# Softmax row sums folded by VectorE in 32-blocks instead of a running PSUM sum, in a one-core attention and FFN kernel

## The chip, the cores and the metric

The program runs on one core of one Trainium2 chip. The time is the device time of one execution in microseconds, the median of three runs. The engines are TensorE (PE, its weight loads are PEld), VectorE (DVE), ScalarE (ACT), GpSimd (POOL) and SyncE (SP, which issues the DMAs). Each engine executes its own instructions strictly in program order and waits for the others through semaphores.

## What is computed

One transformer layer over 2048 tokens of width 512, with 16 heads whose query and key have a 128-wide part without position and a 64-wide part with rotary position. All is float32.

```python
scores = jnp.einsum('bhqd,bhkd->bhqk', q_full, k_full) * scale
scores = jnp.where(causal, -jnp.inf, scores)
attn = jax.nn.softmax(scores.astype(jnp.float32), axis=-1)
out = jnp.einsum('bhqk,bhkd->bhqd', attn, v)
out = out.transpose(0, 2, 1, 3).reshape(b, s, H * DV)
x = _layernorm(x + out @ w_o.T)
x = _layernorm(x + ffn(x))          # w = weight * scale_weight[:, None];  x @ w.T + bias
```

The change concerns the denominator of the softmax: for each query the sum over its keys of the exponentials.

## The kernel before

The attention is worked off in 64 iterations `it`: 4 groups of 4 heads, and in each group the 16 query tiles of 128 tokens. An iteration visits `keys(it)` key tiles (1 to 16, causal), 544 in all. One visit is a slot. In a slot the data of four heads stand side by side: a tile has 128 partitions, which are the keys, and 4 x 128 columns, which are head and query. So a sum over keys is a sum over partitions and over the slots of the iteration.

A slot passes these steps, each on its engine:

- `scores`: five PE matmuls of 512 columns into one of two PSUM banks (`SCORES`, drawn as `rows`). PE may start slot n only when slot n - 2 has gone through `max`.
- `max` (steps `masked`, `max_of`): ACT copies the scores to a ring in SBUF (`pool`, L1606), and after that DVE joins them to a running maximum `top` (L1858). For the first slot of an iteration DVE adds the causal mask instead (L1847).
- `shift`: DVE adds the negated row maximum (L1873), `exp`: ACT (L1611).
- `sum` (`add_up`): DVE adds the exponentials to the running sum in PSUM bank `TOTAL` (L1885; a copy in the first slot, L1882).
- `hi`, `lo`: ACT (L1618) and POOL (L1730) split the exponentials into two parts, `values`: three PE matmuls of 512 columns (L1494, L1495, L1497) add them, times the values, to the bank `OUT`.

The values of a slot come six slots or more after its scores. Around the end of an iteration, `e` being the slot of its last values, there follow once per iteration: ACT copies `TOTAL` to SBUF (`copy_sum`, L1630); PE turns it by four 128x128 transposes (`turn_sum`, L1505); DVE reduces the turned tile over keys to 4 columns (L1889) and takes the reciprocal (L1892); PE spreads it back over the partitions by four more transposes of a broadcast column (`spread_sum`, L1513); DVE multiplies the output by it (`normalise`, L1897); ACT and POOL split the result (L1636, L1735); and 12 PE matmuls project it (`y`, L1527), whose result DVE adds to a partial sum in SBUF (L1836). The row maximum has a like pair of steps, `turn_max` (L1473) and `spread_max` (L1484). The projections of the queries (`q`, L1427, and `pe`, L1440) are made between the slots, for two iterations at a time.

The order on every engine comes from one list `STEPS`. `timetable()` gives each step a slot and a phase within the slot, and `plan()` sorts them and pulls forward what a step waits for. The results of `q`, `pe`, `y`, `turn_max`, `turn_sum`, `spread_sum` and of the two FFN products take turns in the `N_AUX` shared PSUM banks: a use waits until the readers of the use `N_AUX` places earlier are done. The FFN of a query tile follows in the last group, from slot `W_SLOT` on, nine or seven slots behind its last values.

Of the kernel before, what the change touches and what calls it, by code (L numbers as in the profile page):

```python
# [11 lines left out]
ALU = mybir.AluOpType  # L12
# [3 lines left out]
P = 128  # L16
# [646 lines left out]
N_SCORES, N_AUX = 2, 3  # L663
# [106 lines left out]
def timetable():  # L770

    for it in range(N_ITER):
# [55 lines left out]
def readers(use):  # L828
# [11 lines left out]
    if use[0] == "turn_sum":  # L840
        return [("reduce_sum", use[1])]
    if use[0] == "spread_sum":
        return [("normalise", use[1]), ("o_hi", use[1]), ("o_lo", use[1])]
# [16 lines left out]
def waits_for(step):  # L860
# [28 lines left out]
    elif what == "sum":  # L889
        yield ("exp", it, *rest)  # L890
        if it and rest[0] == 0:
            yield ("copy_sum", it - 1)
# [10 lines left out]
    elif what == "copy_sum":  # L903
        yield ("sum", *last_tile(it))
        if it:
            yield ("turn_sum", it - 1)
# [6 lines left out]
    elif what == "turn_sum":  # L913
        yield ("copy_sum", it)
    elif what == "reduce_sum":
        yield ("turn_sum", it)
        if it >= 2:
            yield ("spread_sum", it - 2)
    elif what == "spread_sum":
        yield ("reduce_sum", it)  # L920
# [96 lines left out]
AUX_USES = ("q", "pe", "y", "turn_max", "turn_sum", "spread_sum", "turn", "linear")  # L1017
# [72 lines left out]
def attention_phase(nc, m, block, x, bias, out):  # L1090


    with ExitStack() as ctx:
# [13 lines left out]
        total = sb("total", [P, 512])  # L1107
# [5 lines left out]
        sums = sb("sums", [P, 4, HG])  # L1113
# [17 lines left out]
        OUT, MAXES, TOTAL = m.bank[5:8]  # L1131
# [23 lines left out]
        sum_copied = sem("sum_copied")  # L1155
        sum_turned = sem("sum_turned")
        sum_done = sem("sum_done")
# [47 lines left out]
        def by_head(view):  # L1205

            return view.rearrange("p (h n) -> p h n", h=HG)

# [176 lines left out]
        def _(pe):  # L1385
            def wait_read(u):
# [9 lines left out]
                elif u[0] == "turn_sum":  # L1396
                    pe.wait_ge(sum_done, u[1] + 1)
# [157 lines left out]
            for what, *at in STEPS:  # L1555
# [10 lines left out]
                elif what == "turn_sum":  # L1566
                    turn_sum(*at)
                elif what == "spread_sum":
                    spread_sum(*at)
# [12 lines left out]
        def _(act):  # L1582
# [84 lines left out]
            for what, *at in STEPS:  # L1667
# [18 lines left out]
                elif what == "copy_out":  # L1686
                    copy_out(*at)
                elif what == "copy_sum":
                    copy_sum(*at)
                elif what == "o_hi":  # L1690
                    out_hi(*at)
# [102 lines left out]
        def _(dve):  # L1794
# [80 lines left out]
            def add_up(it, t):  # L1875
                n = number(it, t)
                dve.wait_ge(exp_done, n + 1)
                if t == 0:
                    if it:
# [152 lines left out]
```

## Time and profile before

| | |
|---|---|
| Median of three runs | 1715.34 us (1714.08 to 1717.51) |
| Profiled execution, its span from first to last instruction | 1714.7 us; it has no time of its own beside its span |
| PE busy | 1679.9 us, 98% |
| PEld busy | 1395.8 us, 81% |
| DVE busy | 1380.5 us, 81% |
| ACT busy | 1120.8 us, 65% |
| POOL busy | 979.7 us, 57% |

Busy times are unions: two instructions that overlap count once. Matmuls and DVE operations are pipelined, so a row's duration is longer than the distance to the next row's start. What an instruction takes of its engine is that distance, not its duration.

### The profile page before, as it was taken

The page shows a single profiled execution, that of the slowest core. Times are in us where ns is not written, and L with a number is a line of the kernel's source. Part 1 is how long each engine was busy: PE and PEld are TensorE (multiplying, and loading weights), DVE is VectorE, ACT ScalarE, POOL GpSimd, SP SyncE. Part 2 cuts the span into 40 slices and gives each one's busy share as a digit, 9 for nine tenths or more (in the row PEclk, how much of TensorE's full clock was granted, in tenths as well). Part 3 has the DMA queues.
Part 4 walks back from the last instruction along what each step waited for, and adds up shares of the span by engine and source line. Part 5 has one row for each costly group of instructions (what it writes and reads, how often), then busy time and mean ns, then how long its engine had stood idle before and what let it go on. Part 6 is the DMA issues. An engine that isn't in the chain of part 4 may idle for free.

```text
span 1714.7 us, 28541 instructions
## 1 busy us (share of the span) xinstructions
PE 1679.9 (98%) x8789; PEld 1395.8 (81%) x8789; DVE 1380.5 (81%) x2493; ACT 1120.8 (65%) x2128; POOL 979.7 (57%) x937
## 2 busy tenths in 40 slices
PE   7999999999999999999999999999999999999997
PEld 5567888888888888888888888888888888888775
DVE  3665788888888887878788888888888888888984
ACT  3564676666666676666677666766667777676774
POOL 4333465565555555655566555555556665556785
PEclk9999999999999999999999999999999999999999
DMA  7984322212321412223211413123123111111422
GB/s 204 367 330 136 105 68 62 87 56 88 110 80 37 144 36 81 69 80 117 81 62 44 142 50 92 51 80 114 62 66 105 56 57 62 50 44 44 136 92 80
DMA packets 112175, 164.03 MB, mean 96 GB/s; under 512 B 13600, under 2 KB 83488, under 8 KB 109984
## 3 DMA queue, kind: packets, MB, share of 16 engines
q1 hardware_dynamic: 105296, 125.86, 22.9%
q0 software_dynamic: 4864, 16.26, 3.0%
q10 hardware_dynamic: 1872, 20.19, 2.9%
q8 instruction: 68, 1.11, 0.3%
q14 instruction: 75, 0.61, 0.1%
HBM read 101.19 MB, written 61.08 MB: 95 GB/s over the span
## 4 chain that ended last, share of the span: by engine, by line
PE 89%; POOL 3%; DVE 3%; issue 2%; DMA 1%; ACT 1%; DVEq 0%; SPq 0%; ACTq 0%; POOLq 0%
PE rows L1464 35%; PE bank L1494 7%; PE bank L1497 7%; PE bank L1495 7%; PE rows L1527 7%; PE rows L1427 5%; PE bank L1527 3%; PE rows L392 2%; PE rows L1440 2%; PE bank L1427 2%; PE bank L1484 2%; PE bank L1440 1%; POOL split_p L1730 1%; PE rows L1473 1%; PE rows L1505 1%
## 5 line engine op out<-in xcount | busy, mean ns | idle before, releaser
L1730 POOL TENSOR_TENSOR split_p<-pool,split_p 128x512 fp32r<-128x512 f32 x544 | 703.3, 1294 | 503.2 <-ACT split_p L1618 503.1
L1464 PE MATMUL rows<-q_c,key_c 128*128 128x512 f32 x1632 | 477.0, 400 | 1.4 <-DVE top L1858 1.4
L1606 ACT COPY pool<-rows 128x512 f32<-128x512 f32 x480 | 281.8, 587 | 227.3 <-PE rows L1464 226.6
L1858 DVE TENSOR_TENSOR top<-rows,top 128x512 f32<-128x512 f32 x420 | 288.6, 687 | 124.5 <-ACT pool L1606 121.0
L1873 DVE TENSOR_TENSOR pool<-bank,pool 128x512 f32<-128x512 f32 x544 | 369.7, 680 | 19.8 <-PE bank L1484 19.8
L1611 ACT ACTIVATE pool<-pool 128x512 f32<-128x512 f32 x544 | 345.9, 636 | 18.1 <-DVE pool L1873 17.1
L1618 ACT CAST split_p<-pool 128x512 fp32r<-128x512 f32 x544 | 333.2, 612 | 16.7 <-PE bank L1497 16.7
L1464 PE MATMUL rows<-q_pe,key_pe 128*128 128x512 f32 x1088 | 337.1, 391 | 0.4 <-DMA q_pe<-pe_dram 0.4
L1885 DVE TENSOR_TENSOR bank<-bank,pool 128x512 f32<-128x512 f32 x480 | 330.9, 689 | 0.0
L1464 PEld LDWEIGHTS rows<-q_c,key_c 128*128 128x128 f32 x1632 | 288.0, 189 | 50.0 <-DVE top L1858 5.0
L1464 PEld LDWEIGHTS rows<-q_pe,key_pe 128*128 128x128 f32 x1088 | 204.2, 188 | 46.2 <-DMA q_pe<-pe_dram 0.9
L1497 PE MATMUL bank<-split_p,val 128*128 128x512 f32 x544 | 213.7, 393 | 2.9 <-POOL split_p L1730 2.7
L1494 PE MATMUL bank<-split_p,val 128*128 128x512 f32 x544 | 214.0, 393 | 1.5 <-ACT o_sum L1624 1.0
L1495 PE MATMUL bank<-split_p,val 128*128 128x512 f32 x544 | 212.3, 390 | 0.0
L1527 PE MATMUL rows<-wo,o_t 128*128 128x512 f32 x528 | 127.3, 390 | 0.4 <-ACT o_t L1636 0.4
L1497 PEld LDWEIGHTS bank<-split_p,val 128*128 128x128 f32 x544 | 102.1, 188 | 29.0 <-POOL split_p L1730 7.4
L1494 PEld LDWEIGHTS bank<-split_p,val 128*128 128x128 f32 x544 | 102.1, 188 | 25.9 <-ACT o_sum L1624 3.4
L1735 POOL TENSOR_TENSOR o_t<-o_sum,o_t 128x512 fp32r<-128x512 f32 x64 | 83.0, 1296 | 69.8 <-ACT o_t L1636 69.8
L1495 PEld LDWEIGHTS bank<-split_p,val 128*128 128x128 f32 x544 | 102.2, 188 | 21.2
L1527 PEld LDWEIGHTS rows<-wo,o_t 128*128 128x128 f32 x528 | 98.9, 188 | 21.7 <-issue 1.2
L1636 ACT CAST o_t<-o_sum 128x512 fp32r<-128x512 f32 x64 | 39.7, 621 | 111.4 <-DVE o_sum L1897 97.2
L1427 PE MATMUL rows<-cq,wq 128*128 128x256 f32 x612 | 80.1, 285 | 0.3 <-DVE key_pe L611 0.3
(193 smaller groups left out, 2101.9 us busy)
## 6 DMA issues: line engine op xcount, KB each, us to landing
q_pe<-pe_dram SPq DMA_DIRECT2D x128, 128.0 KB, 2.6
y_dram<-y SPq DMA_DIRECT2D x62, 256.0 KB, 2.1
cq<-cq_dram SPq DMA_DIRECT2D x19, 768.0 KB, 4.9
y<-y_dram SPq DMA_DIRECT2D x48, 256.0 KB, 3.0
pe_dram<-by_sin SPq DMA_DIRECT2D x32, 256.0 KB, 2.1
pe_dram<-by_cos SPq DMA_DIRECT2D x32, 256.0 KB, 2.2
cq_more<-cq_dram SPq DMA_DIRECT2D x10, 768.0 KB, 4.9
table<-table_dram SPq DMA_DIRECT2D x56, 128.0 KB, 2.7
```

What stands on the lines that cost most here:

```text
L1464: mm = pe.matmul(by_head(out), k, q, start=(z == 0), stop=(z == 4))
L1494: pe.matmul(OUT, m.val[:, 0, j, :], split_p[:, n % 2, 0, :], start=(t == 0), stop=False)
L1495: pe.matmul(OUT, m.val[:, 1, j, :], split_p[:, n % 2, 0, :], start=False, stop=False)
L1497: pe.matmul(OUT, m.val[:, 0, j, :], split_p[:, n % 2, 1, :], start=False, stop=(t == keys(it) - 1)).then_inc(values_done, 1)
L1527: mm = pe.matmul(aux(u), o_t[:, a, h * P:h * P + P], m.wo[:, b, h, :], start=(n == 0), stop=(n == 3 * HG - 1))
L1606: nc.scalar.copy(slot(n), SCORES[n % N_SCORES]).then_inc(scores_copied, 1)
L1611: nc.scalar.activation(slot(n), slot(n), ACT.Exp).then_inc(exp_done, 1)
L1618: nc.scalar.copy(split_p[:, n % 2, 0, :], slot(n)).then_inc(p_hi, 1)
L1730: nc.gpsimd.tensor_tensor(split_p[:, n % 2, 1, :], slot(n), stored(split_p[:, n % 2, 0, :]), ALU.subtract).then_inc(p_lo, 1)
L1858: nc.vector.tensor_tensor(out, SCORES[n % N_SCORES], slot(number(it, 0)) if t == 1 else out, ALU.max).then_inc(scores_maxed, 1)
L1873: nc.vector.tensor_tensor(slot(n), MAXES, slot(n), ALU.add).then_inc(shifted, 1)
L1885: nc.vector.tensor_tensor(TOTAL, TOTAL, slot(n), ALU.add).then_inc(summed, 1)
```

## The change

The running sum in PSUM is gone. `add_up` now reduces each tile at once. With `apply_transpose=True` the operation turns every 32x32 block of the tile and sums over what were the block's 32 partitions. A 128x512 tile thus becomes 128x16: partition 32a + i, column b holds the sum over the 32 keys of quarter a for query column 32b + i. These land in `parts`, one row of 16 for every slot of the iteration. At the iteration's end `reduce_sum` adds the rows of the slots to 128x16. One PE product with the 0/1 matrix `fold`, 16 moving columns, adds the four quarters and leaves the total in all four (`fold_sum`). DVE takes the reciprocal of 16 columns and spreads it to 128x512 in the same PSUM bank by a transpose in 32-blocks of the broadcast columns (`spread_sum`). `normalise` is as before but follows directly. `copy_sum` on ACT and the eight transposes on PE are gone. `y` is due at slot e + 3, before at e + 5. `TOTAL`'s bank becomes a fourth shared bank. `fold` is made once, from the identity.

```diff
-N_SCORES, N_AUX = 2, 3
+N_SCORES, N_AUX = 2, 4
...
-        yield e, COPIES, ("copy_sum", it)
+        yield e, COPIES, ("reduce_sum", it)
         yield e + 1, COPIES, ("copy_out", it)
-        yield e, USE_AT, ("turn_sum", it)
-        yield e + 3, USE_AT, ("spread_sum", it)
-        yield e + 5, USE_AT, ("y", it)
+        yield e, USE_AT, ("fold_sum", it)
+        yield e + 3, USE_AT, ("y", it)
...
+    if use[0] == "fold_sum":
+        return [("spread_sum", use[1]), ("normalise", use[1]), ("o_hi", use[1]), ("o_lo", use[1])]
...
-            def turn_sum(it):
-                u = ("turn_sum", it)
+            def fold_sum(it):
+                u = ("fold_sum", it)
                 shared(u)
-                pe.wait_ge(sum_copied, it + 1)
-                for h in range(HG):
-                    mm = pe.transpose(aux(u)[:, h * P:h * P + P], total[:, h * P:h * P + P], m.ident[:, :])
-                mm.then_inc(sum_turned, 1)
-
-            def spread_sum(it):
-                u = ("spread_sum", it)
-                shared(u)
-                pe.wait_ge(inv_done, it + 1)
-                for h in range(HG):
-                    mm = pe.transpose(aux(u)[:, h * P:h * P + P], inv_sum[it % 2][:, h:h + 1].broadcast_to([P, P]),
-                                      m.ident[:, :])
-                mm.then_inc(sum_spread, 1)
+                if it == 0:
+                    pe.wait_ge(fold_made, 2)
+                pe.wait_ge(sum_reduced, it + 1)
+                pe.matmul(aux(u)[:, 0:4 * HG], fold[:, :], row_sum[it % 2], start=True, stop=True).then_inc(sum_folded, 1)
...
-            def copy_sum(it):
-                act.wait_ge(summed, finished(it))
-                if it:
-                    act.wait_ge(sum_turned, it)
-                nc.scalar.copy(total[:, :], TOTAL).then_inc(sum_copied, 1)
...
-                if t == 0:
-                    if it:
-
-                        dve.wait_ge(sum_copied, it)
-                    nc.vector.tensor_copy(TOTAL, slot(n)).then_inc(summed, 1)
-                else:
-                    dve.wait_ge(summed, n)
-                    nc.vector.tensor_tensor(TOTAL, TOTAL, slot(n), ALU.add).then_inc(summed, 1)
+                if t == 0 and it:
+                    dve.wait_ge(sum_reduced, it)
+                nc.vector.tensor_reduce(parts[:, t, :], in_blocks(slot(n)), AX.X, ALU.add, apply_transpose=True
+                                        ).then_inc(summed, 1)
 
             def reduce_sum(it):
-                dve.wait_ge(sum_turned, it + 1)
-                nc.vector.tensor_reduce(row_sum[it % 2], by_head(aux(("turn_sum", it))), AX.X, ALU.add
-                                        ).then_inc(sum_done, 1)
-                dve.wait_ge(sum_done, it + 1)
-                nc.vector.reciprocal(inv_sum[it % 2], row_sum[it % 2]).then_inc(inv_done, 1)
+                dve.wait_ge(summed, finished(it))
+                if it >= 2:
+
+                    dve.wait_ge(sum_folded, it - 1)
+                nc.vector.tensor_reduce(row_sum[it % 2], parts[:, 0:keys(it), :].rearrange("p t b -> p b t"), AX.X, ALU.add
+                                        ).then_inc(sum_reduced, 1)
+
+            def spread_sum(it):
+                u = ("fold_sum", it)
+                dve.wait_ge(sum_folded, it + 1)
+                nc.vector.reciprocal(inv_sum[it % 2], aux(u)[:, 0:4 * HG]).then_inc(inv_done, 1)
+                dve.wait_ge(inv_done, it + 1)
+                nc.vector.transpose(in_blocks(aux(u)),
+                                    inv_sum[it % 2].rearrange("p (b n) -> p b n", n=1).broadcast_to([P, 4 * HG, 32])
+                                    ).then_inc(sum_spread, 1)
```

Two places in the order, both at the end of iteration 16, which has 14 key tiles. On DVE before, the last running sums, the reduction of the turned tile, and three slots later `normalise` (L1897). L1858 is `max`, L1873 `shift`, L1885 and L1882 `sum`:

```order
L1858 TENSOR_TENSOR top<-rows,top 128x512 [waits scores_maxed,scores_copied]
L1873 TENSOR_TENSOR pool<-bank6,pool 128x512
L1885 TENSOR_TENSOR bank7<-bank7,pool 128x512 [waits summed,exp_done]
L1889 TENSOR_REDUCE sums<-rows 128x4 [waits sum_turned]
L1892 RECIPROCAL sums<-sums 128x4 [waits sum_done]
L1858 TENSOR_TENSOR top<-rows,top 128x512 [waits scores_maxed,scores_copied]
...
L1885 TENSOR_TENSOR bank7<-bank7,pool 128x512 [waits summed,exp_done]
L1897 TENSOR_TENSOR o_sum<-bank4,o_sum 128x512 [waits out_copied,sum_spread]
L1858 TENSOR_TENSOR top<-rows,top 128x512 [waits scores_maxed,scores_copied]
```

The same place on DVE in the changed kernel, where L1835 is `max`, L1850 `shift`, L1857 `sum`, L1865 `reduce_sum`, L1871 and L1873 `spread_sum`, L1880 `normalise`:

```order
L1835 TENSOR_TENSOR top<-rows,top 128x512 [waits scores_maxed,scores_copied]
L1865 TENSOR_REDUCE sums<-parts 128x16 [waits sum_folded,summed]
L1850 TENSOR_TENSOR pool<-bank7,pool 128x512
L1857 TENSOR_REDUCE parts<-pool 128x16 [waits sum_reduced,exp_done]
L1835 TENSOR_TENSOR top<-rows,top 128x512 [waits scores_maxed,scores_copied]
L1850 TENSOR_TENSOR pool<-bank7,pool 128x512
L1857 TENSOR_REDUCE parts<-pool 128x16 [waits exp_done]
L1871 RECIPROCAL sums<-bank5 128x16 [waits sum_folded]
L1873 STREAM_TRANSPOSE bank5<-sums 128x512 [waits inv_done]
L1880 TENSOR_TENSOR o_sum<-bank5,o_sum 128x512 [waits out_copied,sum_spread]
L1835 TENSOR_TENSOR top<-rows,top 128x512 [waits scores_maxed,scores_copied]
```

The reduction of the slots has moved one slot ahead, and in place of two operations ahead of a `max` there are now three, `normalise` among them, which stood three slots later.

On PE before, `turn_sum` (L1505) stands behind the last values, `spread_sum` (L1513) three slots later:

```order
L1497 MATMUL bank5<-split_p,val 128x512 [waits p_lo]
L1505 MATMUL rows<-ident,total 128x128 [waits sum_copied,rope_parts]
L1505 MATMUL rows<-ident,total 128x128 x3
L1464 MATMUL rows<-q_c,key_c 128x512 [waits scores_maxed]
...
L1497 MATMUL bank5<-split_p,val 128x512 [waits p_lo]
L1513 MATMUL bank4<-ident,sums 128x128 [waits inv_done,max_done]
L1513 MATMUL bank4<-ident,sums 128x128 x3
L1464 MATMUL rows<-q_c,key_c 128x512 [waits scores_maxed]
```

On PE in the changed kernel (L1493 is the last matmul of `values`, L1502 `fold_sum`, L1460 `scores`, L1514 `y`):

```order
L1493 MATMUL bank6<-split_p,val 128x512 [waits p_lo]
L1502 MATMUL bank5<-sums,fold 128x16 [waits sum_reduced,max_done]
L1460 MATMUL rows<-q_c,key_c 128x512 [waits scores_maxed]
...
L1493 MATMUL bank6<-split_p,val 128x512 [waits p_lo]
L1514 MATMUL rows<-wo,o_t 128x512 [waits o_hi,wo_loaded,rope_parts]
```

One matmul of 16 columns stands where four transposes stood, nothing stands for the second four, and the projection follows three slots of scores and values behind the fold.

## Rows read from the trace of the kernel before

**Rows 1.** The page: busy shares of the engines, and TensorE's clock in slices.

```profile
PE 1679.9 (98%) x8789; PEld 1395.8 (81%) x8789; DVE 1380.5 (81%) x2493; ACT 1120.8 (65%) x2128; POOL 979.7 (57%) x937
...
PEclk9999999999999999999999999999999999999999
```

**Rows 2.** Busy time by stretch, with counts: the steady part, then the end.

```profile
180.00:1598.00 1418.00, 1417.19 (x7460) 1204.58 (x7459) 1199.07 (x2021) 957.96 (x1777) 830.33 (x671) 1.00 0.24 76
...
1598.00:1715.00 117.00, 97.61 (x473) 76.07 (x471) 86.28 (x197) 72.91 (x124) 85.58 (x156) 0.98 0.25 83
```

**Rows 3.** The same stretch for L1505, L1513 (PE, PEld), L1885, L1882 (DVE) alone.

```profile
180.00:1598.00 1418.00, 34.70 (x232) 28.61 (x232) 1.00 0.24 76
...
180.00:1598.00 1418.00, 34.69 (x232) 28.26 (x232) 1.00 0.24 76
...
180.00:1598.00 1418.00, 319.89 (x464) 1.00 0.24 76
...
180.00:1598.00 1418.00, 40.28 (x59) 1.00 0.24 76
```

**Rows 4.** Timeline of PE behind iteration 16: start, us, line, count.

```profile
600.47 0.84 PE L1464 MATMUL rows<-q_c,key_c 128*128 128x512 f32 x3
601.15 0.62 PE L1464 MATMUL rows<-q_pe,key_pe 128*128 128x512 f32 x2
...
602.28 0.60 PE L1513 MATMUL bank<-ident,sums 128*128 128x128 f32 x4
602.63 0.94 PE L1464 MATMUL rows<-q_c,key_c 128*128 128x512 f32 x3
603.41 0.62 PE L1464 MATMUL rows<-q_pe,key_pe 128*128 128x512 f32 x2
```

**Rows 5.** Timeline of PE in the preparation: float32 products of 64 columns.

```profile
20.39 1.00 PE L402 MATMUL bank<-pool,x_t 128*128 128x64 f32 x8
21.23 2.00 PE L436 MATMUL bank<-pool 128*128 128x128 f32 x16
```

**Rows 6.** Timeline of DVE behind iteration 16.

```profile
596.95 0.69 DVE L1858 TENSOR_TENSOR top<-rows,top 128x512 f32<-128x512 f32 x1 [0.37 <-ACT pool L1606]
597.56 0.68 DVE L1873 TENSOR_TENSOR pool<-bank,pool 128x512 f32<-128x512 f32 x1
598.15 0.69 DVE L1885 TENSOR_TENSOR bank<-bank,pool 128x512 f32<-128x512 f32 x1
598.75 0.68 DVE L1889 TENSOR_REDUCE sums<-rows 128x4 f32<-128x512 f32 x1
599.47 0.18 DVE L1892 RECIPROCAL sums<-sums 128x4 f32<-128x4 f32 x1
599.56 0.68 DVE L1858 TENSOR_TENSOR top<-rows,top 128x512 f32<-128x512 f32 x1
```

**Rows 7.** Timelines at the first and the last of the tight places, and at one wide one.

```profile
224.91 0.67 DVE L1858 TENSOR_TENSOR top<-rows,top 128x512 f32<-128x512 f32 x1
...
225.64 0.98 PE L1464 MATMUL rows<-q_c,key_c 128*128 128x512 f32 x3
...
1540.54 0.68 DVE L1858 TENSOR_TENSOR top<-rows,top 128x512 f32<-128x512 f32 x1
...
1541.68 0.84 PE L1464 MATMUL rows<-q_c,key_c 128*128 128x512 f32 x3
...
779.89 0.67 DVE L1858 TENSOR_TENSOR top<-rows,top 128x512 f32<-128x512 f32 x1
...
781.41 2.27 PE L1427 MATMUL rows<-cq,wq 128*128 128x256 f32 x17
```

**Rows 8.** The chain of work that ended last, in order of time: the end.

```profile
1599.81 1.28 POOL split_p L1730
...
1655.19 0.20 POOL ffn_small L1751
...
1664.53 0.44 PE bank L1505 x4
```

More of the change, by code:

```diff
@@ L839, in readers @@
         return [("reduce_max", use[1])]
[L840 to L843, printed above, removed]
+    if use[0] == "fold_sum":
+        return [("spread_sum", use[1]), ("normalise", use[1]), ("o_hi", use[1]), ("o_lo", use[1])]
     if use[0] == "y":
@@ L891, in waits_for @@
         if it and rest[0] == 0:
-            yield ("copy_sum", it - 1)
+            yield ("reduce_sum", it - 1)
     elif what == "lo":
@@ L902, in waits_for @@
             yield ("o_lo", it - 2)
-    elif what == "copy_sum":
-        yield ("sum", *last_tile(it))
-        if it:
-            yield ("turn_sum", it - 1)
     elif what == "turn_max":
@@ L912, in waits_for @@
             yield ("spread_max", it - 8)
-    elif what == "turn_sum":
-        yield ("copy_sum", it)
     elif what == "reduce_sum":
-        yield ("turn_sum", it)
+        yield ("sum", *last_tile(it))
         if it >= 2:
-            yield ("spread_sum", it - 2)
+            yield ("fold_sum", it - 2)
+    elif what == "fold_sum":
+        yield ("reduce_sum", it)
     elif what == "spread_sum":
-        yield ("reduce_sum", it)
+        yield ("fold_sum", it)
     elif what == "normalise":
@@ L1016 @@
 PROJECTION_STEPS = [("q", N_PAIR - 1, 0), ("q", N_PAIR - 1, 1)]
-AUX_USES = ("q", "pe", "y", "turn_max", "turn_sum", "spread_sum", "turn", "linear")
+AUX_USES = ("q", "pe", "y", "turn_max", "fold_sum", "turn", "linear")
 def plan():
@@ L1106, in attention_phase @@
         top = sb("top", [P, 2, 512])
-        total = sb("total", [P, 512])
+        fold = sb("fold", [P, P])
+        parts = sb("parts", [P, NT, 4 * HG])
+        sums = sb("sums", [P, 4, 4 * HG])
         y = sb("y", [P, 2, HID])
@@ L1112, in attention_phase @@
         stats = m.small[:, 20:20 + 8 * HG].rearrange("p (b h) -> p b h", b=8)
-        sums = sb("sums", [P, 4, HG])
         row_sum = [sums[:, b, :] for b in range(2)]
@@ L1130, in attention_phase @@
         SCORES, AUX = m.bank[0:N_SCORES], m.bank[N_SCORES:N_SCORES + N_AUX]
-        OUT, MAXES, TOTAL = m.bank[5:8]
+        OUT, MAXES = m.bank[6:8]
         wq_loaded = sem("wq_loaded")
@@ L1154, in attention_phase @@
         out_copied = sem("out_copied")
-        sum_copied = sem("sum_copied")
-        sum_turned = sem("sum_turned")
-        sum_done = sem("sum_done")
+        sum_reduced = sem("sum_reduced")
+        sum_folded = sem("sum_folded")
+        fold_made = sem("fold_made")
         inv_done = sem("inv_done")
@@ L1207, in by_head, with in_blocks @@
             return view.rearrange("p (h n) -> p h n", h=HG)
+        def in_blocks(view):
+            return view.rearrange("p (b n) -> p b n", n=32)
         def by_pair(view):
@@ L1395, in wait_read @@
                     pe.wait_ge(max_done, u[1] + 1)
-                elif u[0] == "turn_sum":
-                    pe.wait_ge(sum_done, u[1] + 1)
                 elif u[0] == "turn":
@@ L1565, in _ @@
                     values(*at)
[L1566 to L1569, printed above, removed]
+                elif what == "fold_sum":
+                    fold_sum(*at)
                 elif what == "q":
@@ L1687, in _ @@
                     copy_out(*at)
-                elif what == "copy_sum":
-                    copy_sum(*at)
                 elif what == "o_hi":
@@ L1896, in normalise @@
                 dve.wait_ge(out_copied, it + 1)
-                nc.vector.tensor_tensor(o_sum[:, it % 2, :], aux(("spread_sum", it)), o_sum[:, it % 2, :], ALU.mult
+                nc.vector.tensor_tensor(o_sum[:, it % 2, :], aux(("fold_sum", it)), o_sum[:, it % 2, :], ALU.mult
                                         ).then_inc(normalised, 1)
@@ L1946, in copy_mask, with make_fold @@
                 dve.wait_ge(mask_copied, 1)
+            def make_fold():
+                nc.vector.tensor_reduce(fold[:, 0:32], m.ident[:, :].rearrange("p (a i) -> p i a", i=32), AX.X, ALU.add
+                                        ).then_inc(fold_made, 1)
+                dve.wait_ge(fold_made, 1)
+                nc.vector.tensor_copy(fold[:, 32:P].rearrange("p (a i) -> p a i", i=32),
+                                      fold[:, 0:32].rearrange("p (a i) -> p a i", a=1).broadcast_to([P, 3, 32])
+                                      ).then_inc(fold_made, 1)
             for what, *at in STEPS:
@@ L1961, in _ @@
                         copy_mask()
+                        make_fold()
                     masked(at[0])
@@ L1972, in _ @@
                     reduce_sum(*at)
+                elif what == "spread_sum":
+                    spread_sum(*at)
                 elif what == "normalise":
```

1 line of the change is left out of this document (removed).

## The prediction

> **What bounds the kernel now.** I read the page first: PE is busy for 98% of the span, the others for 81% or less, and the granted clock is in its top tenth in every slice [rows 1]. Then the table by stretch. From 180 to 1598 us PE is busy for 1417.2 of 1418.0 us at a granted clock of 1.00, which is the upper level, 2.4 GHz. DVE is busy for 1199.1 of them, ACT for 958, POOL for 830 [rows 2]. So in this stretch every nanosecond taken off PE shortens the kernel, as long as no other engine makes PE wait. Behind it, from 1598 us on, PE is busy for 97.6 of 117.0 us. The chain that ended last runs through POOL from 1599.8 to 1655.4 us and comes back to PE after that [rows 8]. What PE saves between those two points is worth nothing.
>
> Where the margin of the other engines lies I read in the timeline, since the 81% of DVE is an average. In a plain slot PE needs eight matmuls of 512 columns. Three of them start 0.68 us ahead of the fourth (600.47 to 601.15), 0.227 us each, so a slot is 1.82 us [rows 4]. DVE does `max`, `shift` and `sum` in it. Each lasts 0.68 or 0.69 us, but they start 0.60 us apart [rows 6]. That makes 1.80 us: in a run of plain slots DVE is as full as PE, and only the projections and transposes on PE between the slots let it catch up.
>
> **What goes from PE.** The two blocks of four transposes per iteration. A block starts 0.35 us ahead of the next matmul (602.28 to 602.63), and the three matmuls behind it take 0.78 us in place of 0.68 (602.63 to 603.41) [rows 4]. A block thus costs 0.45 us. In the stretch there are 232 transposes of each kind, 58 blocks each [rows 3]: 116 x 0.45 = 52.2 us.
>
> **What comes to PE.** 58 products of 16 columns in the stretch. The trace has none of 16 columns. The nearest is a float32 product of 64: eight in 0.84 us (20.39 to 21.23), 0.105 us each [rows 5]. Each of them loads other weights, as this one does, so I take 0.11 us. The bounds are zero and 0.45, a whole block of today. 58 x 0.11 = 6.4 us (0 to 26).
>
> The Trainium skill (TensorE: Matmul & The Clock Gate, the table in cycle terms) gives a product of 1 to 64 columns some 60 cycles, about 25 ns. By that, as an estimate, the term would be 1.5 us. The rows contradict it here, since consecutive products with new weights stand 0.105 us apart.
>
> **What changes on DVE.** 523 sums in the stretch, 464 as additions and 59 as copies [rows 3], become reductions with a transpose, which the trace doesn't show. The nearest row is the plain reduction of a 128x512 tile, 0.68 us like an addition [rows 6]. All 512-column operations shown here start 0.60 us apart whatever they read and write, so I see no gain from reading one operand less, and take 0.60 again. Upward the bound is a second pass over the tile, 1.20 us. That end is a rival below.
>
> Rule and row again differ in size only. The Trainium skill (VectorE: DVE Perf Modes, the three transpose paths) has 311 ns for a 128-column transpose in 32-blocks. By the formula of its errata section, (128 + 151) / 0.96 = 291 ns, a plain operation takes 20 ns less. As an estimate that adds 0.02 us per sum, 11 us of DVE and, at the twenty places below, about 2 us of the end. Another rule of that page speaks against the change: it calls `tensor_reduce` the slowest operation of the engine and advises against it on a hot path. The trace doesn't bear that out, the reduction lasts 0.68 and the addition 0.69 us [rows 6].
>
> Per iteration DVE loses the reduction of the turned tile and a reciprocal, 0.81 us together (598.75 to 599.56) [rows 6]. It gets a reduction of `parts`, 16 to 256 columns: between 0.1 (the reciprocal's distance) and 0.6, taken as 0.3. It also gets a reciprocal of 16 columns, about 0.25 with the wait for its own result, and a transpose of 512 columns, about 0.72 with such a wait (598.75 to 599.47 is this case) [rows 6]. That is 0.46 us more per iteration, 27 us in the stretch: DVE 1226 of then about 1380 us, 89%. Not yet the bound on average. ACT loses one copy per iteration, which nothing waits for.
>
> **What the moved steps do.** This is the term that the averages hide. PE's `scores` of slot n wait for DVE's `max` of slot n - 2. Today the reduction and the reciprocal stand ahead of such a `max`. In the changed order it is the reciprocal, the transpose and `normalise`: 0.25 + 0.72 + 0.60 = 1.57 us in place of 0.81, so this `max` ends 0.76 us later. PE comes there 0.45 - 0.11 = 0.34 us earlier, because its block ahead of this point has shrunk. Together 1.10 us of margin are used.
>
> I measured today's margin at all 58 places, PE's start less the end of `max`, and added the idle time that DVE had just ahead of the `max`. Behind iteration 16 `max` ends at 600.24 and PE starts at 600.47, 0.23 us [rows 4, 6]. The first tight place has 0.06 us (225.58 to 225.64), the last 0.46 (1541.22 to 1541.68) [rows 7]. At 20 of the 58 places the margin is below 1.0 us, together 9.3 us short of it. At the others it is 1.0 to 4 us, because a projection or a block stands between, as at 781.41 [rows 7]. For 1.10 us the shortfall is 9.3 + 20 x 0.10 = 11.3 us. PE can't make up what it waits. The small reduction of `parts` stands one slot ahead, where DVE idles 0.37 us [rows 6], and goes in there. Without any of these stalls this term is 0. With a sum 0.1 us dearer, some four sums in a row without a gap eat 0.4 us more at each of 20 places, +8 us. Further waits, on the fourth shared bank or on `y`, I put at nothing. A use has more banks for fewer uses (64 fewer), and `y` stands three slots, 5.5 us, behind the fold, with 2 us of DVE work and two splits of ACT and POOL ahead of it.
>
> **The end.** Of the 12 blocks behind 1598 us, five come when PE is back on the chain, as at 1664.53 [rows 8]: 5 x 0.34 = 1.7 us. The chain from the last sums to the output loses a copy and gains a transpose. I take -2 us, with -8 (four banks relieve the FFN's products of PE's 19 idle us [rows 2]) and +3 as the ends.
>
> **Sum**, on the span of the profiled execution: 1714.7 - 52.2 + 6.4 + 11.3 - 2 = 1678.2 us. The median of the runs is 0.6 us above that span, so I forecast 1679 us.
>
> **The rivals.**
>
> *All of the saving comes through.* If DVE has more slack than the places show, or the transpose starts while the reciprocal drains, the 11.3 us fall away: 1668 us. For it: PE waits for DVE practically never today. Against it: the 20 tight places. 13%.
>
> *DVE makes PE wait at more places.* A reduction at 0.70 us gives slots of 1.90 us against PE's 1.82, +8 us, and more places become tight, or the fold costs nearer to a block: 1697 to 1710 us. 12%.
>
> *The reduction with a transpose costs two passes, and DVE becomes the bound: slower.* At 0.60 us more per sum DVE has 1226 + 523 x 0.60 = 1540 us of work in the stretch, against 1418 today: +122 us. About 20 sums behind it add up to 12 us. That gives 1715 + 122, 1837 us, or somewhat more with DVE's unavoidable waits. It decides against the change from (1418 - 1226) / 523 = 0.37 us per sum on, a reduction of 0.97 us. For it: no row shows this operation, and turning a block means to collect 32 columns first. Against it: the collecting can run ahead, and other DVE operations all stream one column per step. 16%.
>
> *The change doesn't gain.* The stalls spread to all places with under 2 us of margin and take back all that PE saves, within 0.2% of 1715. 4%.
>
> The forecast itself, 1665 to 1697 us, has 55%.
>
> **How the numbers follow.** A measurement of this kernel can tell 0.2%, 3.4 us, from no change. Faster is the forecast, the full saving and the added waits: 55 + 13 + 12 = 80%. Same is 4%, slower 16%. The range of 1658 to 1708 us holds the first three: below, full saving, fold at nothing and the better end (1668 - 6 - 6 = 1656); above, the forecast with a fold at a half block and a dearer sum (1679 + 7 + 8) and more waits. What lies outside is the slow reduction and the lost gain.
>
> **What would show it.** In the changed profile PE should still be busy for 97% or more. The gap from the fold to the next `scores` and what they lose should sum to 0.11 us. The reductions `parts<-pool` should start 0.60 us ahead of the next operation. PE's waits for `top` behind `spread_sum` should sum to about 11 us, in pieces of 0.1 to 1 us. I am wrong if the reductions stand 0.9 us or more apart from what follows, if PE's idle time in the steady part is above 30 us, or if those waits are missing.

## The result and the profile after

The changed kernel takes 1771.38 us in the median of four runs (1768.14 to 1773.64), against 1716.42 us before in the same series. The ratio is 1.032, with a 95% interval of 1.0304 to 1.0336. I had forecast 1679 us with a range of 1658 to 1708, so the sign was wrong. The profiled execution has a span of 1769.0 us.

The page of the changed kernel: busy times, and from its costliest groups the scores on PE and the new reduction on DVE (busy time, mean ns of one, idle time just ahead and its releaser).

```profile
PE 1663.8 (94%) x8405; PEld 1364.8 (77%) x8405; DVE 1414.2 (80%) x2559; ACT 1094.5 (62%) x2064; POOL 977.8 (55%) x937
...
L1460 PE MATMUL rows<-q_c,key_c 128*128 128x512 f32 x1632 | 478.6, 402 | 44.7 <-DVE top L1835 44.2
...
L1857 DVE TRANSPOSE_TENSOR_REDUCE parts<-pool 128x16 f32<-128x512 f32 x544 | 380.1, 699 | 0.2
```

PE is busy for 16 us less than before and still ends 54 us later. Before, its share was 98% [rows 1]; now it is 94%. DVE is at 80%, no fuller than it was, so it is no new bound on average. In the table by stretch (busy time of PE, PEld, DVE, ACT and POOL, then granted clock and DMA) the loss lies in the steady part:

```profile
180.00:1649.00 1469.00, 1402.12 (x7098) 1174.78 (x7098) 1226.14 (x2075) 932.90 (x1716) 827.20 (x670) 0.99 0.23 73
1649.00:1769.00 120.00, 96.29 (x443) 74.33 (x441) 90.56 (x205) 70.56 (x119) 86.79 (x156) 0.95 0.25 82
```

PE idles 66.9 us of 1469 where it idled 0.8 of 1418 [rows 2]. The end has hardly changed: PE is busy for 96.3 of 120 us, against 97.6 of 117. The waits of PE and of its weight loads name the engine that is late (us in total, times, longest):

```profile
PEld rows L1460 <- DVE top L1835: 55.3, 38, 2.8
PE rows L1460 <- DVE top L1835: 44.2, 34, 2.4
...
PEld bank L1493 <- POOL split_p L1707: 23.3, 40, 2.1
PE bank L1493 <- POOL split_p L1707: 10.5, 14, 1.4
PE bank L1469 <- DVE top L1835: 8.0, 4, 2.6
...
PE rows L1469 <- DVE top L1835: 5.0, 3, 1.7
```

Both the scores (L1460) and `turn_max` (L1469) wait for `max` (L1835). These waits are what I had foreseen, but the 44.2 us of the scores alone are four times as much as my 11.3, and with the 13.0 of `turn_max` it is five times. PE and PEld rows of one line are largely the same waits seen twice, so they are not added.

### The profile page after: what moved, and what is told of

It reads as the page before. It is cut to its first block, busy times and chain, and to the rows that moved or that the text cites. A ratio compares the mean times of both kernels' runs of the same rounds, so it can differ in the third digit from the quotient of the medians.

```text
span 1769.0 us, 27228 instructions
## 1 busy us (share of the span) xinstructions
PE 1663.8 (94%) x8405; PEld 1364.8 (77%) x8405; DVE 1414.2 (80%) x2559; ACT 1094.5 (62%) x2064; POOL 977.8 (55%) x937
## 4 chain that ended last, share of the span: by engine, by line
PE 70%; DVE 16%; issue 5%; ACT 4%; POOL 3%; DMA 1%; ACTq 0%; DVEq 0%; SPq 0%; POOLq 0%
PE rows L1460 26%; PE rows L1514 6%; PE bank L1493 5%; PE bank L1491 5%; PE bank L1490 5%; PE bank L1423 4%; PE bank L1514 4%; DVE top L1835 3%; PE rows L1423 3%; DVE parts L1857 3%; ACT pool L1591 2%; PE rows L392 2%; PE rows L1436 2%; DVE pool L1850 2%; DVE o_sum L1880 2%
## 5 line engine op out<-in xcount | busy, mean ns | idle before, releaser
L1460 PE MATMUL rows<-q_c,key_c 128*128 128x512 f32 x1632 | 478.6, 402 | 44.7 <-DVE top L1835 44.2
L1591 ACT COPY pool<-rows 128x512 f32<-128x512 f32 x480 | 281.5, 587 | 275.1 <-PE rows L1460 274.4
L1835 DVE TENSOR_TENSOR top<-rows,top 128x512 f32<-128x512 f32 x420 | 284.0, 676 | 134.4 <-ACT pool L1591 132.7
L1850 DVE TENSOR_TENSOR pool<-bank,pool 128x512 f32<-128x512 f32 x544 | 369.3, 679 | 15.9 <-PE bank L1480 15.8
L1857 DVE TRANSPOSE_TENSOR_REDUCE parts<-pool 128x16 f32<-128x512 f32 x544 | 380.1, 699 | 0.2
L1460 PEld LDWEIGHTS rows<-q_c,key_c 128*128 128x128 f32 x1632 | 289.6, 189 | 106.8 <-DVE top L1835 55.3
L1460 PE MATMUL rows<-q_pe,key_pe 128*128 128x512 f32 x1088 | 339.1, 393 | 0.0
L1460 PEld LDWEIGHTS rows<-q_pe,key_pe 128*128 128x128 f32 x1088 | 205.2, 189 | 45.8 <-DMA q_pe<-pe_dram 0.3
L1493 PE MATMUL bank<-split_p,val 128*128 128x512 f32 x544 | 216.9, 399 | 10.5 <-POOL split_p L1707 10.5
L1493 PEld LDWEIGHTS bank<-split_p,val 128*128 128x128 f32 x544 | 102.9, 189 | 44.0 <-POOL split_p L1707 23.3
L1615 ACT CAST o_t<-o_sum 128x512 fp32r<-128x512 f32 x64 | 39.6, 619 | 151.3 <-DVE o_sum L1880 125.5
L1514 PE MATMUL rows<-wo,o_t 128*128 128x512 f32 x492 | 119.3, 391 | 0.0
L1514 PEld LDWEIGHTS rows<-wo,o_t 128*128 128x128 f32 x492 | 92.7, 189 | 19.1
L1514 PE MATMUL bank<-wo,o_t 128*128 128x512 f32 x276 | 71.6, 411 | 0.2 <-ACT o_t L1615 0.2
```

Of the source, the lines that this page charges most:

```text
L1460: mm = pe.matmul(by_head(out), k, q, start=(z == 0), stop=(z == 4))
L1493: pe.matmul(OUT, m.val[:, 0, j, :], split_p[:, n % 2, 1, :], start=False, stop=(t == keys(it) - 1)).then_inc(values_done, 1)
L1514: mm = pe.matmul(aux(u), o_t[:, a, h * P:h * P + P], m.wo[:, b, h, :], start=(n == 0), stop=(n == 3 * HG - 1))
L1591: nc.scalar.copy(slot(n), SCORES[n % N_SCORES]).then_inc(scores_copied, 1)
L1835: nc.vector.tensor_tensor(out, SCORES[n % N_SCORES], slot(number(it, 0)) if t == 1 else out, ALU.max).then_inc(scores_maxed, 1)
L1850: nc.vector.tensor_tensor(slot(n), MAXES, slot(n), ALU.add).then_inc(shifted, 1)
```

## Where the time goes at one place

The timeline of DVE behind iteration 16, the place of [rows 4, 6] (start, us, and idle time before with its releaser):

```profile
609.49 0.70 DVE L1850 TENSOR_TENSOR pool<-bank,pool 128x512 f32<-128x512 f32 x1
610.09 0.71 DVE L1857 TRANSPOSE_TENSOR_REDUCE parts<-pool 128x16 f32<-128x512 f32 x1
610.70 0.24 DVE L1871 RECIPROCAL sums<-bank 128x16 f32<-128x16 f32 x1
610.98 0.73 DVE L1873 STREAM_TRANSPOSE bank<-sums 128x512 f32<-128x512 f32 x1
611.74 0.69 DVE L1880 TENSOR_TENSOR o_sum<-bank,o_sum 128x512 f32<-128x512 f32 x1
613.60 0.69 DVE L1835 TENSOR_TENSOR top<-rows,top 128x512 f32<-128x512 f32 x1 [1.17 <-ACT pool L1591]
```

The same place on ACT:

```profile
609.52 0.61 ACT L1603 CAST split_p<-pool 128x512 fp32r<-128x512 f32 x1
612.46 0.62 ACT L1615 CAST o_t<-o_sum 128x512 fp32r<-128x512 f32 x1 [2.33 <-DVE o_sum L1880]
612.98 0.58 ACT L1591 COPY pool<-rows 128x512 f32<-128x512 f32 x1
```

And on PE:

```profile
608.31 0.29 PE L1502 MATMUL bank<-sums,fold 128*128 128x16 f32 x2
608.45 0.94 PE L1460 MATMUL rows<-q_c,key_c 128*128 128x512 f32 x3
609.22 0.63 PE L1460 MATMUL rows<-q_pe,key_pe 128*128 128x512 f32 x2
...
611.95 0.39 PE L1493 MATMUL bank<-split_p,val 128*128 128x512 f32 x1
614.34 0.96 PE L1460 MATMUL rows<-q_c,key_c 128*128 128x512 f32 x3 [2.00 <-DVE top L1835]
...
616.38 2.92 PE L1514 MATMUL rows<-wo,o_t 128*128 128x512 f32 x12
```

The triple on DVE is about as long as I had costed it: 610.70 to 612.34, counting 0.60 us for `normalise`, so 1.64 us in place of 1.57. DVE could start `max` at 612.34. It starts it at 613.60. What `max` needs is ACT's copy of the scores (L1591), and ahead of that copy ACT's program has `o_hi` (L1615), which waits for `normalise`. ACT stands still for 2.33 us, the last 0.8 of them with the scores ready in their bank (the matmuls that write them end at 611.67). So the delay isn't DVE's alone. It is a loop through two engines: triple, `o_hi`, copy, `max`, scores. It costs 1.26 us on top of the 0.87 us of my sum (1.10 less the margin of 0.23), together 2.13. PE stands idle for 2.00 us.

The kernel before had `o_hi` ahead of the copy too. There PE had the `y` block to do at that moment. Its timeline on PE:

```profile
606.41 2.77 PE L1527 MATMUL rows<-wo,o_t 128*128 128x512 f32 x11
```

and on DVE:

```profile
606.79 0.69 DVE L1858 TENSOR_TENSOR top<-rows,top 128x512 f32<-128x512 f32 x1 [1.17 <-ACT pool L1606]
```

It is the same 1.17 us of idle DVE, behind `normalise` at e + 4, but under 2.8 us of `y` at e + 5. In the changed kernel `normalise` stands at e + 1 and `y` at e + 3. The distance has grown from one slot to two, and `y` starts only at 616.38, behind the scores that waited.

## The experiments

All ratios are against the kernel before, timed beside the experiment. Where a kernel has a line more in the order's planner, its line numbers are one higher: L1461 is scores, L1494 the last values, L1515 `y`, L1836 `max`.

**The whole group late, as before** (e1_late_group).

```diff
-        yield e, USE_AT, ("fold_sum", it)
-        yield e + 3, USE_AT, ("y", it)
+        yield e + 3, USE_AT, ("fold_sum", it)
+        yield e + 5, USE_AT, ("y", it)
```

> The changed kernel with the fold at slot e + 3 and the projection y at e + 5, so that fold, reciprocal, transpose, normalise and the splits stand where normalise stood before the change. Theory (place): the loss comes from DVE's normalise and, behind it in ACT's order, the split o_hi, which hold up ACT's copy of the next scores and so the next max at a point where PE has no other work ahead of the scores that wait for it. At the late place y follows before those scores, and the stalls of 1.5 to 2.7 us should be gone: 1660 to 1675 us, the granted clock back at 0.99 or more. Rival (price): the new operations on DVE cost too much wherever they stand: 1740 to 1770 us.

Measured: 1725.51 us, 1.0069 (1.0052 to 1.0086), span 1722.7. The waits of the scores for `top` were down to 1.4 us, as expected, 46 us came back, and still it missed the expected range by 50 us. The waits that took their place:

```profile
PE rows L1514 <- ACT o_t L1615: 17.8, 30, 1.7
...
PE bank L1490 <- ACT o_sum L1609: 13.1, 8, 2.5
```

Where the triple now stands, `normalise` stood alone before. The triple is 1.04 us longer (1.64 less 0.60), and now `y`, one slot behind it, waits for `o_hi`. The second line is the first matmul of `values`, which waits for ACT's copy of the finished `OUT` bank. So 1 us of delay in this chain lands on `y` here, where the changed kernel has it on the scores.

**ACT's split behind `max`** (e2_split_behind_max): `o_hi` and `o_lo` no longer stand ahead of the copy for which `max` waits.

```diff
-            at.setdefault((n + 1, READ), []).append(reader)
+            phase = MAX + 0.5 if reader[0] in ("o_hi", "o_lo") else READ
+            at.setdefault((n + 1, phase), []).append(reader)
```

> The changed kernel in which the splits o_hi (ACT) and o_lo (POOL) come behind the copy and the max of the same slot; DVE's order is untouched. Theory (link through ACT): the stall at iteration 16 was 2.2 us, of which 1.25 us is the copy of the scores waiting behind o_hi; some 32 such stalls lose 1.25 us each, 40 us, and with fewer idle pieces the clock keeps its upper level, about 10 to 15 us more: 1700 to 1725 us, with stalls of 0.5 to 1 us left. Rival (DVE alone, as the prediction had it): ACT's order doesn't matter, 1760 to 1775 us.

Measured: 1730.39 us, 1.009 (1.0073 to 1.0107), span 1731.4, 5 us above the expected range. That is 41 us off the changed kernel by ACT's and POOL's order alone, with every instruction on DVE and on PE in the same order as in the changed kernel. The waits of the scores for `top` shrank from 44.2 to 11.0 us. Together with `turn_max`, and counted as in the account below, what PE loses behind a `max` that follows `normalise` falls from 60.8 us at 34 places to 17.0 at 25. At iteration 16 it is 0.90 us, and my sum for DVE alone gives 0.87. But POOL's part of the split now came late:

```profile
PE bank L1494 <- POOL split_p L1708: 27.3, 35, 1.8
PE rows L1461 <- DVE top L1836: 11.0, 25, 0.8
```

**`y` later** (e3_y_late): `y` at e + 5 instead of e + 3, nothing else.

```diff
-        yield e + 3, USE_AT, ("y", it)
+        yield e + 5, USE_AT, ("y", it)
```

> The changed kernel with y alone back at slot e + 5, fold and all else at e as in the change. Theory (place of normalise and o_hi): the stalls come before y and stay, 1760 to 1775 us. Rival (y comes too early and waits for its splits): most of the loss is gone, 1680 to 1700 us.

Measured: 1785.3 us, 1.0411 (1.0394 to 1.0429), span 1783.4. So the changed kernel doesn't lose because `y` waits for its input. With `y` further away it was slower still, 10 us above what I expected. The waits for `top` are no longer than in the changed kernel (39.9 us for the scores). The granted clock of the run is 0.987, and counted as in the account below most of the 14 us is time at the lower clock.

**`y` earlier** (e5_y_two): the same line, with `e + 2`, which puts the block directly between the slot of `normalise` and the scores that wait.

> The changed kernel with y one slot earlier, at e + 2, so that it stands on PE between the end of the values and the scores that wait for the late max. Theory: y's 2.7 us cover the late max; what is left is y's own wait for o_hi, about 0.9 us at each of some 32 places: 1705 to 1725 us. Rival (any early place is bad, the nearer the worse, since y then waits for the whole chain): 1770 us or more.

Measured: 1699.06 us, 0.9908 (0.9892 to 0.9925), span 1697.1, 6 us below the range that I expected. One number in one line is worth 72 us, and the kernel is now 0.9% faster than before. No `max` behind `normalise` makes PE wait any more. What remained was `y`'s own wait for `o_hi`:

```profile
PE bank L1514 <- ACT o_t L1615: 14.6, 20, 1.6
PE rows L1514 <- ACT o_t L1615: 9.1, 19, 0.9
```

**The spreading transpose left out** (e4_no_spread). The kernel leaves out the spread: 16 columns are copied, and `normalise` reads a bank of which the rest isn't written.

```diff
-                nc.vector.transpose(in_blocks(aux(u)), ... broadcast_to([P, 4 * HG, 32])
-                                    ).then_inc(sum_spread, 1)
+                nc.vector.tensor_copy(aux(u)[:, 0:4 * HG], inv_sum[it % 2]).then_inc(sum_spread, 1)
```

> The changed kernel with the transpose that spreads the reciprocals over 512 columns left out: in its place stands a copy of the 16 reciprocals, so that normalise multiplies by wrong numbers and the output is not that of the reference. Order and waits are the same. Theory: the group ahead of the late max is 0.5 us shorter, and at some 30 stalls that is 15 us, with some of the lower clock 20 to 30 us: 1738 to 1755 us. If the transpose were the cause by itself, the loss against before would be gone: 1670 to 1700 us.

Measured: 1736.82 us, 1.0121 (1.0104 to 1.0138), span 1735.8, 1 us below the expected range. The copy takes 0.21 us where the transpose took 0.76 (start to next start), and the kernel gains 35 us, so the loss against before isn't the transpose's alone. Counted as in the account below, the waits for `top` behind `normalise` fall from 60.8 to 42.7 us, by 0.5 us at each of some 34 places. The lower clock gives back about 10 us more. The rest lies in smaller waits.

**The old kernel with its own steps moved** (e7_before_moved): does the place alone cost it?

```diff
-        yield e + 3, USE_AT, ("spread_sum", it)
-        yield e + 5, USE_AT, ("y", it)
+        yield e + 1, USE_AT, ("spread_sum", it)
+        yield e + 4, USE_AT, ("y", it)
```

> The kernel before, with none of the new operations; only the times in the timetable are changed: spread_sum at slot e + 1 in place of e + 3 and y at e + 4 in place of e + 5. normalise and o_hi then stand in a slot behind which PE has two slots of scores and values, and no y, ahead of the scores that wait for that slot's max. Theory (place): about 1.1 us of stall at each of some 30 places, and pieces at the lower clock: 1740 to 1765 us, though PE, DVE and ACT do the same work. Rival (price of the new operations): the place doesn't matter, 1710 to 1720 us.

Measured: 1773.34 us, 1.034 (1.0323 to 1.0358), span 1769.9. The time, 8 us above the expected range, looks like support, but the waits say it is another thing: the transposes of `spread_sum` on PE come too early for the reciprocal.

```profile
PE rows L1513 <- DVE sums L1892: 27.0, 31, 2.4
PE bank L1513 <- DVE sums L1892: 9.8, 15, 1.1
```

So this run says nothing about the place of `normalise`. I repeated it one slot later, with `y` left at e + 5 (e10_before_spread_two):

```diff
-        yield e + 3, USE_AT, ("spread_sum", it)
+        yield e + 2, USE_AT, ("spread_sum", it)
```

> The kernel before with spread_sum at slot e + 2 in place of e + 3 and nothing else changed, y stays at e + 5. The earlier move to e + 1 had brought a wait of its own (PE for the reciprocal, 37 us) and so told nothing about the place; here PE comes one slot after the reciprocal. normalise and o_hi move one slot ahead, and no y stands on PE between them and the scores that wait for that slot's max. Theory (place, link through ACT): about 1 us at each of some 30 places, in waits of the scores for top, and some of the lower clock: 1740 to 1760 us. Rival (only the new operations on DVE are too dear): 1710 to 1720 us.

Measured: 1753.15 us, 1.0215 (1.0199 to 1.0231), span 1750.7, as expected. Now the waits are of the kind of the changed kernel, a third as long, with the old operations:

```profile
PE rows L1464 <- DVE top L1858: 14.7, 29, 1.3
PEld rows L1464 <- DVE top L1858: 28.5, 36, 1.7
```

Nothing but the place has changed here: `normalise` at e + 3 and `y` at e + 5, two slots apart as in the change, so that the scores between them are uncovered. That costs 37 us by itself, without any new operation.

**Only `normalise` and the splits late** (e8_normalise_late). The reciprocal and the transpose stay at e + 1, the rest goes back to e + 4, `y` to e + 5.

```diff
-        yield e + 3, USE_AT, ("y", it)
+        yield e + 5, USE_AT, ("y", it)
...
-            at.setdefault((n + 1, READ), []).append(reader)
+            late = 4 if reader[0] in ("normalise", "o_hi", "o_lo") else 1
+            at.setdefault((n + late, READ), []).append(reader)
```

> The changed kernel with normalise, o_hi and o_lo at slot e + 4 and y at e + 5, where they stood before the change; fold, reciprocal and the transpose stay at e and e + 1. Theory: at e + 1 DVE has 0.97 us ahead of the max in place of 0.81, which uses 0.5 us of margin with PE's earlier arrival, some 1 to 3 us of stalls in all; at e + 4 all is as before, and y doesn't wait for a chain through reciprocal and transpose as it did with the whole group late. 1663 to 1680 us. Rival (the fourth bank is held for four slots, or the pieces still collide): 1690 us or more.

Measured: 1706.46 us, 0.995 (0.9933 to 0.9968), span 1705.6. That is 26 us above the expected range. The table by stretch, here of PE alone, shows a steady part nearly without idle time that reaches a like point 28 us earlier than before, and an end that is 18 us longer, part of it at the lower clock:

```profile
180.00:1570.00 1390.00, 1381.70 (x7095) 1.00 0.24 77
1570.00:1705.00 135.00, 104.07 (x452) 0.91 0.24 78
```

The fold's bank is held until `normalise`, now three slots longer, and at the end the FFN's products (L1523, L1535) and `y` wait for banks that `normalise` frees. The longest waits of that stretch:

```profile
PE rows L1515 <- DVE o_sum L1881: 3.8, 1, 3.8
PE bank L1535 <- DVE o_sum L1881: 3.8, 1, 3.8
PE bank L1523 <- DVE o_sum L1881: 3.4, 1, 3.4
```

**The group a phase earlier and `y` at e + 2** (e9_group_ahead). DVE does the group ahead of `shift` and `sum` of slot e + 1 instead of behind them, so that it is past when `max` comes.

```diff
-        yield e + 3, USE_AT, ("y", it)
+        yield e + 2, USE_AT, ("y", it)
...
-            at.setdefault((n + 1, READ), []).append(reader)
+            phase = SHIFT - 0.5 if reader[0] in ("spread_sum", "normalise") else READ
+            at.setdefault((n + 1, phase), []).append(reader)
```

> The changed kernel with y at e + 2 and reciprocal, transpose and normalise ahead of the shift and the sum of slot e + 1 instead of behind them. With y at e + 2 alone y waited 0.8 us at some 40 places for its first split. Theory: the group ends 1.2 us earlier, y's wait goes: 1670 to 1685 us. Rival: the shift, 1.7 us later, makes exp, the splits and so the values late, PE waits for POOL's split instead: 1695 us or more.

Measured: 1669.67 us, 0.9736 (0.972 to 0.9753), span 1667.3. This beats both kernels and lies at the lower end of the expected range. In the steady part (columns as above) PE has next to no idle time left:

```profile
180.00:1553.00 1373.00, 1367.99 (x7075) 1166.43 (x7075) 1218.40 (x2068) 932.72 (x1711) 826.73 (x668) 1.00 0.24 77
```

The timeline of DVE behind the same kind of place in this kernel, then ACT, then PE:

```profile
586.18 0.69 DVE L1881 TENSOR_TENSOR o_sum<-bank,o_sum 128x512 f32<-128x512 f32 x1
586.79 0.68 DVE L1851 TENSOR_TENSOR pool<-bank,pool 128x512 f32<-128x512 f32 x1
...
588.05 0.69 DVE L1836 TENSOR_TENSOR top<-rows,top 128x512 f32<-128x512 f32 x1
```

```profile
586.91 0.62 ACT L1616 CAST o_t<-o_sum 128x512 fp32r<-128x512 f32 x1 [1.14 <-DVE o_sum L1881]
587.43 0.58 ACT L1592 COPY pool<-rows 128x512 f32<-128x512 f32 x1
```

```profile
587.59 0.39 PE L1494 MATMUL bank<-split_p,val 128*128 128x512 f32 x1
587.82 2.93 PE L1515 MATMUL rows<-wo,o_t 128*128 128x512 f32 x12
590.59 0.84 PE L1461 MATMUL rows<-q_c,key_c 128*128 128x512 f32 x3
```

`o_hi` and the copy run while DVE has `shift` and `sum` to do, and `max` ends at 588.74 under a `y` block that lasts until 590.59.

**The two parts apart** (e12_ahead_y_three): e9 with `y` back at e + 3.

> The fast version with y back at e + 3, as the change has it, so that only the place of the DVE group within slot e + 1 differs from the change. o_hi then ends before ACT's copy of the scores would start and delays it little, but the max still comes behind reciprocal, transpose and normalise, and no y stands ahead of the scores that wait for it. Theory: what remains is the term of the prediction, DVE's delay alone, 0.5 to 1 us at 20 to 30 places: 1685 to 1705 us. Rival (the link through ACT was all): 1668 to 1675 us.

Measured: 1718.24 us, 1.0013 (1.0004 to 1.0022), span 1716.0, 13 us above what I expected. Its waits:

```profile
PE rows L1461 <- DVE top L1836: 17.5, 33, 1.2
...
PEld rows L1461 <- DVE top L1836: 28.4, 34, 1.6
```

ACT's copy now holds up only 8 of the 64 `max` behind `normalise` by more than 0.5 us, against 52 in the changed kernel. Still PE waits at 33 places, 26.8 us in all: there DVE's own lateness, without the link through ACT, is enough.

With the changed kernel, e5, e12 and e9 there are all four cases:

| | `y` at e + 3 | `y` at e + 2 |
|---|---|---|
| group behind `sum` | 1771.38 | 1699.06 |
| group ahead of `shift` | 1718.24 | 1669.67 |

The place of `y` is worth 72 us in the one row and 49 in the other, the place of the group 53 and 29. Both work against the same late chain, so the second to come is worth less. What is left for it differs. With `y` at e + 2 no wait for the late `max` remains, and the group's 29 us are mostly `y`'s wait for `o_hi` (14.6 and 9.1 us in e5, next to nothing in e9). With the group ahead, 27 of `y`'s 49 us are waits for `top`.

**The fourth bank** (e11_ahead_three_banks): e9 with `N_SCORES, N_AUX = 2, 3`.

> The fast version (y at e + 2, the DVE group ahead of shift and sum of slot e + 1) with three shared banks in place of four. What the fourth bank is worth: theory, nothing in the steady part, up to 5 us at the end, where the FFN's products take turns with y and the folds: 1668 to 1676 us. Rival (the fourth bank carries a part of the gain): 1680 us or more.

Measured: 1675.7 us, 0.9763 (0.9749 to 0.9776), span 1673.8. The fourth bank is worth 6 us in this order, about the 5 that I had allowed it.

## Why the prediction was wrong

**What goes from PE** was right. The page has 384 matmuls less (8789 to 8405): 512 transposes gone, 128 matmuls come.

**What comes to PE** was mis-sized. The lines of the changed kernel, kept apart by shape, for the fold, the spread and the reduction of the slots (the last in one of its shapes, 16 slots):

```profile
L1502 PE MATMUL bank<-sums,fold 128*128 128x16 f32 x88 | 12.8, 221 | 0.2 <-DVE sums L1865 0.2
L1502 PE MATMUL rows<-sums,fold 128*128 128x16 f32 x40 | 6.0, 226 | 3.8 <-DVE sums L1865 3.8
...
L1873 DVE STREAM_TRANSPOSE bank<-sums 128x512 f32<-128x512 f32 x44 | 32.0, 727 | 1.5
L1865 DVE TENSOR_REDUCE sums<-parts 128x16 f32<-128x256 f32 x4 | 2.3, 586 | 0.0
```

The 64 folds appear as 128 matmuls, two to a fold. At iteration 16 the fold starts 0.14 us ahead of the scores (608.31 to 608.45), and the three matmuls behind it take 0.77 us in place of 0.68. That is 0.23 us per fold, where I had 0.11: 7 us more over the steady part, within my bounds.

**What changes on DVE** was right, all of it. The reduction with a transpose lasts 0.70 us and starts 0.61 us ahead of what follows (610.09 to 610.70), where I had taken 0.60. The rival of two passes, 1837 us, is dead. The reciprocal takes 0.28 us to the transpose, the transpose 0.76 to `normalise`, for which I had 0.25 and 0.72.

The Trainium skill (VectorE: DVE Perf Modes, Rules for kernel authors) calls `tensor_reduce` the slowest operation of the engine. This case's traces don't agree for tiles of this size: the new reductions take 699 ns of mean, the additions that they replace (L1885) took 689.

**What the moved steps do** is the step that failed: its 11.3 us of stalls measured some 80. Three of its statements were wrong.

- "So this `max` ends 0.76 us later." That counts only DVE. The `max` also needs a copy by ACT, which stood behind `o_hi`, which waited for the moved `normalise`. That adds 1.26 us at iteration 16, and e2, which moves nothing but the two splits, gives back 41 us. I had looked in the order for what stands behind `normalise` on DVE, and not for what stands behind its reader on ACT.
- "At the others it is 1.0 to 4 us, because a projection or a block stands between." In the changed kernel PE waits for a `max` behind `normalise` at 34 of the 64 places, not at 20, and loses 60.8 us there. Of my 20 tight places 18 are among them, with 36.2 us, 2.0 each where the sum had 0.6. The other 16 bring 24.6 us. Not every block is cover: at six of them `turn_max` itself waits for the same `max` (13.6 us). And cover can move away: at six more, PE was in a `y` block before when this `max` ended. With `y` put into the new gap, at e + 2, 72 us come back (e5).
- "Further waits, on the fourth shared bank or on `y`, I put at nothing." On the bank this was right as far as tested: in the order of e9, e11 gives the fourth bank a gain of 6 us. What I priced for `y` was its wait for its input; what it cost was the cover that it had been for others.

e10 confirms it without any new operation: the old kernel with this group one slot nearer to the last values loses 37 us.

A second loss followed from the first. In the table by stretch, PE alone (busy, granted clock, DMA):

```profile
408.00:412.00 4.00, 1.45 (x12) 1.00 0.21 70
412.00:416.00 4.00, 4.00 (x19) 0.57 0.46 144
```

In the first stretch PE waited for `top` for 2.55 us; in the second it is busy throughout at a granted clock of 0.57, mostly the lower level of 1.2 GHz. There are nine such pieces at 1.2 GHz ahead of 1650 us in the changed kernel, and none there in the kernel before. Each follows right behind a wait for `top` of 1.8 to 2.6 us. The reverse doesn't hold: of the eight waits of 1.8 to 2.0 us only three have such a piece behind them, of the six of 2.3 us and more all have. Behind the 2.00 us of iteration 16 the granted clock stays at 1.00.

**The account.** I took for each line of matmuls its usual distance from start to start, and summed from 180 us on what single distances exceed it by, if by more than 0.15 us, with the pieces at the lower clock counted apart. The places above and in e2, e4 and e12 are counted in the same way, by what the first matmul behind the `max` exceeds its usual distance. Stalls come to 15.2 us before, 94.9 after, 16.3 in e9; the lower clock costs 14.8 us after, and nothing before or in e9. The sum of 110 us is firm. How it divides is not: counting the instructions at the edges of the pieces the other way moves some 6 us from the stalls to the clock. PE's work shrinks by 64 x 2 x 0.45 = 57.6 less 64 x 0.225 = 14.4, so 43.2 us. Then 1714.7 - 43.2 + 79.7 + 14.8 = 1766.0 us, against a span of 1769.0. For e9 it is 1714.7 - 43.2 + 1.1 = 1672.6 against 1667.3, and e11, which has no fourth bank, is at 1673.8. In place of my 11.3 us of stalls there were some 80, and the clock on top, for which the sum had no term. The waits for `top` of 60.8 us are the greater part. The rest are mainly waits for POOL's and ACT's splits.

**The rivals.** "DVE makes PE wait at more places" named the right engine and the wrong cause: it had a dearer reduction, which didn't come, and its price of 1697 to 1710 us left out the link through ACT, most of the other places and the clock. The full saving, 1668 us, is what e9 reaches. None had the convoy through ACT. My own sign of error, more than 30 us of idle PE in the steady part, is what the trace shows: 66.9.

Left open: how much e2 would have gained without the later waits for POOL's split, why e12 lies 13 us above what I expected, and what exactly the last 120 us owe to each step.

## What to carry to other kernels

When a step moves, follow its result through every in-order engine: what stands behind its readers there waits too, and may be what the next critical step needs. A margin belongs to the blocks that lie in it, so count it after the move, without those that have moved away or that wait for the same thing themselves. Put a long block that needs nothing from the late chain into the gap, and try that place by itself: here one slot was worth 49 to 72 us, more than the operations saved.

## What the runs showed of the hardware

A float32 product of 16 columns appears as two matmuls and costs 0.23 us of PE. A float32 reduction with a 32-block transpose of 128x512 costs nearly what an addition does, 0.61 against 0.60 us to the next start. And nine of the fourteen waits of 1.8 to 2.6 us on PE ahead of 1650 us were followed by a piece at the lower clock (granted clock 0.57 from 412 to 416 us), so such a stall can cost more than its own length: 14.8 us on top of 79.7.
